# Two layers of attention and expert layers: GpSimd waits for the stores of Q and K in front of two kinds of indirect DMA

## What is computed

```python
xn = _layernorm(x, axis=-1)
x = x + _L0_attn_ref(xn, ...) + _L0_ffn_ref(xn, ...)   # experts: relu(xn W1 + b1) W2 + b2
xn = _layernorm(x, axis=-1)
x = x + _L1_attn_ref(xn, ...) + _L1_ffn_ref(xn, ...)   # experts: xn We + be
...
scores = einsum('bhqd,bhkd->bhqk', q, k) / sqrt(HD)    # attention, causal, softmax, times v, times Wo
topk_gates, topk_idx = jax.lax.top_k(gates, K)         # K = 2 of E = 8 experts
```

## Time and profile before

| | us |
|---|---|
| median of 3 executions | 3185.12 (3184.64 to 3189.36) |
| the profiled execution | 3198.38 |
| its span, first to last instruction | 3196.6 |
| PE busy in it | 3013.7 (94%) |
| DVE, ACT, POOL busy | 2392.2, 1981.2, 1024.4 |
| granted TensorE clock, mean share | 0.982 |

### The profile page before, as it was taken

How to read it: one execution, slowest core, us unless ns; L and a number is a source line. 1 busy time by engine, 2 the same in 40 slices (tenths; PEclk the granted TensorE clock), 3 DMA queues, 4 the chain that set the end, 5 groups by cost and what they waited for, 6 DMA issues and landing times.

```text
span 3196.6 us, 62083 instructions
## 1 busy us (share of the span) xinstructions
PE 3013.7 (94%) x19056; PEld 1579.7 (49%) x19056; DVE 2392.2 (75%) x7245; ACT 1981.2 (62%) x4954; POOL 1024.4 (32%) x1244
## 2 busy tenths in 40 slices
PE   5799999999999999999999999999999999999998
PEld 3454544445455554544545555454545555445443
DVE  5676768777786777878777787777877767687784
ACT  2466656666666666666666666666666666666665
POOL 4115134151432413334151331513324142241512
PEclk7899999999999999999999999999999999999999
DMA  6767455363554535446374563635546365453642
GB/s 188 201 169 209 133 157 152 107 195 110 180 184 145 184 122 176 133 130 188 100 216 139 167 182 120 190 97 166 161 132 209 120 192 153 145 156 103 185 135 77
DMA packets 328103, 496.03 MB, mean 155 GB/s; under 512 B 56832, under 2 KB 242656, under 8 KB 327776
## 3 DMA queue, kind: packets, MB, share of 16 engines
q1 hardware_dynamic: 293536, 416.99, 43.7%
q0 software_dynamic: 24576, 67.14, 6.9%
q10 hardware_dynamic: 9664, 7.93, 0.9%
HBM read 344.19 MB, written 152.84 MB: 155 GB/s over the span
## 4 chain that ended last, share of the span: by engine, by line
PE 79%; DVE 10%; issue 4%; ACT 3%; DMA 2%; SPq 1%; POOL 1%; another core or an unknown queue 0%; DVEq 0%; ACTq 0%; POOLq 0%
PE po L1144 16%; PE pmx L1094 15%; PE pst L1081 14%; PE pst L1128 9%; PE pmx L1214 5%; PE pst L1113 5%; PE pst L1225 4%; PE pmx L1183 4%; PE pst L1102 3%; DVE pmx L843 3%; DVE x L975 2%; PE pmx L1162 2%; PE pst L1150 1%; ACT probs L686 1%; DMA xg<-x_slots 1%
## 5 line engine op out<-in xcount | busy, mean ns | idle before, releaser
L686 ACT ACTIVATE probs<-pst 128x512 f32<-128x512 f32 (+3 forms) x3072 | 1402.8, 496 | 450.9 <-PE pst L1081 422.9
L595 POOL TENSOR_SCALAR_AFFINE_SELECT probs<-probs 128x512 f32<-128x512 f32 x512 | 332.5, 650 | 1686.3 <-ACT probs L686 1684.7
L839 DVE TENSOR_REDUCE rmax<-pmx 128x1 f32<-128x512 f32 x1024 | 668.9, 683 | 142.4 <-PE pmx L1094 134.5
L1081 PE MATMUL pst<-qs,k_first 98*128 98x512 bf16 (+3 forms) x2048 | 693.8, 344 | 34.3 <-ACT xgT L691 17.6
L843 DVE CUSTOM_DVE_ANT_0 pmx<-pmx,mask,rmax 128x128 f32<-128x128 f32 (+3 forms) x1024 | 537.5, 556 | 217.2 <-PE pmx L1094 189.0
L1094 PE MATMUL pmx<-k_first,qs 96*128 96x512 bf16 (+2 forms) x2048 | 672.6, 346 | 28.0 <-issue 9.3
L1144 PE MATMUL po<-probs,v 128*32 128x512 f32 (+3 forms) x6144 | 663.5, 504 | 14.6 <-POOL probs L595 10.6
L843 DVE CUSTOM_DVE_ANT_0 pmx<-pmx,mask 128x128 f32<-128x128 f32 (+3 forms) x1024 | 482.8, 510 | 168.1 <-PE pmx L1094 152.8
L1094 PEld LDWEIGHTS pmx<-k_first,qs 96*128 96x128 bf16 x2048 | 199.8, 99 | 377.8 <-issue 172.1
L1094 PE MATMUL pmx<-k_second,qs 96*128 96x128 bf16 (+3 forms) x1024 | 305.9, 303 | 28.3 <-DVE otok L955 14.5
L1081 PE MATMUL pst<-qs,k_second 98*128 98x512 bf16 (+3 forms) x1024 | 302.4, 302 | 5.8 <-issue 3.8
(11 more groups left out here) (121 smaller groups left out, 3379.9 us busy)
## 6 DMA issues: line engine op xcount, KB each, us to landing
wt<-w_tiles SPq DMA_DIRECT2D x161, 513.0 KB
qk_parts<-parts SPq DMA_DIRECT2D x256, 192.0 KB
xg<-x_slots SPq DMA_DIRECT2D x368, 128.0 KB
y_slots<-ys SPq DMA_DIRECT2D x368, 128.0 KB
wt<-w_tiles SPq DMA_DIRECT2D x184, 256.0 KB
qs<-qk_parts SPq DMA_DIRECT2D x128, 192.0 KB
qs<-qk_parts SPq DMA_DIRECT2D x128, 128.0 KB
k_first<-qk_parts SPq DMA_DIRECT2D x64, 192.0 KB, 2.9
```

Of the source, the lines that this page charges most:

```text
L595: pool.affine_select(out=tri, in_=tri, compare_op=ALU.is_ge, fill=0.0, base=0, pattern=[[0, GH], [1, P]], channel_multiplier=-1).then_inc( ...
L686: act.activation(probs[:, u % 2, j, 0:w], ps[:, 0:w], ACT.Exp, scale=DH ** -0.5).then_inc(st_read, 1)
L839: dve.tensor_reduce(rmax0[:, col:col + 1], src, AX_X, ALU.max).then_inc(mx_read, 1)
L1081: pe.matmul(ps[:, 0:w], keys[0:SROWS, j, k % HT * P:(k % HT + 1) * P], qs[0:SROWS, set_no(q, n) % QRING, j, a:a + w], start=True, stop=Tru ...
```

## The change

POOL gets two new waits, and nothing else is changed. In front of the ninth scatter it waits until all stores of tile 1 issued so far have landed, the last of which are the four of the same run's first half. In front of the first gather, in all runs but the last, it waits until all stores of tile 0 issued so far have landed, the last of which are the four of the next run's second half.

```diff
@@ scatter
                     pool.wait_ge(slots_ready, q + 1)
+                if SCATTER[a] == PROJ[0, NP - 1] + 2 and a % 2 == 0:
+                    pool.wait_ge(qk_stored[KD - 1], (q * CH + 1) * 64)
                 pool.indirect_dma_start(
@@ gather
                         pool.wait_ge(y_stored[n], 16 * (last // YRING + 1))
+                if a == 0 and q + 1 < NR:
+                    pool.wait_ge(qk_stored[0], (q + 1) * CH * 64 + 128)
                 need(pool, combined, m - GRING + 1)
```

## The result

| | before | after |
|---|---|---|
| median, us (same chip, 4 executions each) | 3187.24 | 3229.77 |
| range | 3184.64 to 3192.07 | 3223.98 to 3230.84 |
| the profiled execution | 3198.38 | 3230.84 |
| its span | 3196.6 | 3229.1 |

The ratio is 1.0128, with a 95% interval of 1.0110 to 1.0146: 42 us slower. The forecast was 3195 and its range ended at 3212. The sign was right, the size was four times too small. The profiled execution of before lies 11 us above its median and that of after 1 us above, so the two spans differ by 32.5 us where the medians differ by 42.5.

The account below looks back on a forecast made before the run. PE, busy 3013.7 of 3196.6 us, was taken to bound the kernel. The terms 8.0 us (first gather), 0 (ninth scatter, steady state) and 2.0 (start) make 10 us, so the median 3185.1 becomes 3195, range 3184 to 3212.

Parts of the forecast that it names:

- The gather's wait: On POOL in front of the first gather, at fifteen handovers: late masks of unit 44 cost PE 8.0 us together.
- From the landing to the next indirect DMA: On POOL, once the awaited stores have landed: the held gather or scatter was to start 0.15 us later.
- From the end of the issues to the landing: SP's stores of Q and K parts: landed 2.6 us after their issue, with 4.16 us as the other end.
- the slack arithmetic of the prediction: At unit 44's mask: lateness beyond PE's slack is paid in full, 0.36 us in eight handovers and 0.73 in seven.
- The scatter's wait in steady state: On POOL in front of the ninth scatter, after the start: the mask of unit 36 stays in time, costing nothing.
- the cover: POOL's 5.92 us of idle time ahead of unit 36's mask in the second run, claimed to absorb the held scatters.
- The start: Start of the program: the held ninth scatter delays PE's first tokens once, 2.0 us, between 1.3 and 2.8.
- The slack swallows it: Rival, chance 0.26: unit 44's masks are in time or PE's later waits shrink; start plus up to 4 us, 3186.5 to 3191.
- The landing comes with the last issue: Rival, chance 0.05: stores count as landed about when their issue ends, so masks are not late; 3185.
- The long landing: Rival, chance 0.10: stores land 4.16 us after the issues at each handover; 34 us slower, 3219.
- Not slower, a little faster: Rival, chance 0.09: stores and loads get the DMA engines alone, PE's 3.3 us of token waits vanish; -2 us, 3183.
- The bound on the gain: Whole kernel: stores are awaited only once, 2.1 us, in the start; faster loads can gain no more than 3.3 us.

## Why the prediction missed, step by step

**The gather's wait: the right place, 8.0 us instead of 36.** The mechanism is the one forecast, and three of its numbers were too small.

- *From the landing to the next indirect DMA* I took 0.15 us, the idle time of a gather that waited for nothing. In after it is 0.81 to 0.89 us in all fifteen handovers, mean 0.88. The held scatters show 0.74 to 0.75 in fifteen runs and 0.26 once, in the start. The row I chose showed a gather that stood ready behind another instruction, not one that a landing releases.
- *From the end of the issues to the landing* I took 2.6; the mean is 2.86 (2.43 to 3.66). Together the first gather starts 3.74 us after the issues, not 2.75.
- *Four gathers and the mask* take 5.53 us on average, not 5.30, partly because the mask itself took 0.80 in some handovers [compare rows 4].

These make each mask 1.22 us later than worked out. With that, the slack arithmetic of the prediction gives 8 x 1.58 + 7 x 1.95 = 26.3 us; measured at unit 44 are 25.0, in thirteen of the fifteen, 0.2 to 3.2 us each. One reading of the rows was wrong besides: the first and the fifteenth handover stood for two kinds, but the four issues take 3.05 to 4.11 us in the one kind and 2.65 to 3.72 in the other. Handover by handover, the forecast's own numbers give 11.0 us in place of 8.0, and with the 1.22 us added 27.0 in place of 26.3.

- *What follows a late PE* was put at nothing, without a reason. The fourteenth handover, PE, and the same place in windows of time (columns: length, busy time of PE, its loads, DVE, ACT, POOL, then the granted clock, DMA share, GB/s):

```profile
2852.95 1.07 PE L1148 MATMUL po<-probs,v 128*32 128x512 f32 x8
2858.24 1.94 PE L1148 MATMUL po<-probs,v 128*32 128x512 f32 x8 [2.64 <-POOL probs L599]
2861.15 3.34 PE L1218 MATMUL pmx<-xnT,wqk 128*128 128x512 f32 x4
```

```profile
2850.00:2855.00 5.00, 5.00 (x33) 2.35 (x30) 3.07 (x16) 3.47 (x8) 1.95 (x2) 1.00 0.59 165
2855.00:2858.00 3.00, 0.60 (x4) 0.10 (x1) 1.52 (x5) 1.34 (x4) 2.61 (x3) 0.88 0.84 227
2858.00:2861.00 3.00, 2.76 (x13) 0.91 (x14) 1.38 (x7) 0.29 (x1) 2.53 (x4) 0.50 0.95 242
2861.00:2864.00 3.00, 3.00 (x6) 1.31 (x5) 1.71 (x6) 0.46 (x2) 1.45 (x3) 0.50 0.20 49
2864.00:2867.00 3.00, 3.00 (x21) 1.59 (x20) 1.36 (x3) 1.54 (x5) 1.14 (x2) 0.99 0.30 87
```

PE had 0.60 us of work in three, waiting for the mask; then its granted clock stood at 0.50, which is 1.2 GHz instead of 2.4, and the same eight multiplications took 1.94 us where they had taken 1.07. So PE lost the wait and then lost again at half speed. In after, 13.6 us are lost this way at units 44 and 45, in six of the fifteen handovers (a wait of 2.60 us in another one was not followed by it); before had nothing of the kind there. 25.0 + 13.6 = 38.6, and the table has 38.1.

So the step that made the forecast miss is this term of the sum, 8.0 us for the wait in front of the first gather: the landing and the 0.15 us behind it were taken too short, which makes 25.0, and the half clock adds 13.6.

**The scatter's wait in steady state: 0 forecast, 42 lost and 42 given back.** That "nothing" came out near the truth is luck, two terms of 42 us that cancel. The step that failed here is "the cover is that idle time, in which POOL waits for ACT's exponentials". I measured the cover in a trace in which the units just ahead of it run slow, and held it fixed. The ninth run of before, its seventh to tenth scatters, and where PE, ACT and DVE stand around the ninth and tenth:

```profile
1608.49 0.99 POOL L570 DMA_INDIRECT x_slots<-xn,slot  x1 [0.15 <-issue]
1609.78 0.96 POOL L570 DMA_INDIRECT x_slots<-xn,slot  x1 [0.30 <-issue]
1611.05 0.96 POOL L570 DMA_INDIRECT x_slots<-xn,slot  x1 [0.30 <-issue]
1612.32 0.96 POOL L570 DMA_INDIRECT x_slots<-xn,slot  x1 [0.30 <-issue]
```

```profile
1611.26 0.44 PE L1102 MATMUL pst<-ident,xg 128*128 128x128 f32 x2
1611.54 0.22 PE L1094 MATMUL pmx<-k_second,qs 96*128 96x128 bf16 x1
...
1613.46 0.39 PE L1081 MATMUL pst<-qs,k_first 98*128 98x512 bf16 x1 [0.99 <-issue]
...
1615.13 0.39 PE L1081 MATMUL pst<-qs,k_first 98*128 98x512 bf16 x1 [1.06 <-issue]
```

```profile
1613.02 0.39 ACT L691 ACTIVATE xgT<-pst 128x256 f32<-128x256 f32 x1 [1.94 <-PE pst L1081]
```

```profile
1614.39 0.36 DVE L843 CUSTOM_DVE_ANT_0 pmx<-pmx,mask,rmax 128x128 f32<-128x128 f32 x1 [3.66 <-PE pmx L1094]
```

PE turned the tokens from 1611.26 on, 0.44 us, and ACT copies them only at 1613.02; PE did the small product at 1611.54 and DVE takes it at 1614.39. The consumers see PE's results 1.3 to 2.6 us late (counted from PE's ends, which the profile models), and then PE waits for the consumers. The same place in after, where no scatter runs:

```profile
1625.24 0.44 PE L1106 MATMUL pst<-ident,xg 128*128 128x128 f32 x2
```

```profile
1625.72 0.38 ACT L695 ACTIVATE xgT<-pst 128x256 f32<-128x256 f32 x1 [0.65 <-PE pst L1106]
```

0.04 us after PE's end. Of the 42 us at units 34 and 35, 27.2 are idle time of PE and 11.9 half clock. The pointer was in the earlier trace rows, PE's largest named wait, 17.6 us for ACT's `xgT`; I read it as one number of a list and did not ask in which unit it sat. The row is gone, or down to 1.0 us, in every run that frees units 34 and 35, and in the others it stays (14.1 us with the gather's wait alone, 13.3 with that wait at the third gather, 16.4 with waits already passed).

What the scatters need beside them for this has two readings. In all fifteen runs of before the ninth and tenth scatters stand beside the stores, and they also follow the seventh and eighth, which wait for `low_parts`, with only 0.30 us between. Every run that freed units 34 and 35 ended both. The trace of after tells them apart. Take ACT's copies of tokens and its exponentials, without the first of each unit, where ACT was idle before them: they wait for PE alone. In before 22 of 327 start over 1 us after PE's end, 19 of these in unit 34. In after none does in unit 34, but 14 of 36 in unit 36 and 4 of 5 in unit 37, around the four held scatters, and 7 of 26 in unit 44, around the four held gathers, and both go only when the stores have landed. The third run of after, where the landing is at 464.27:

```profile
465.02 0.96 POOL L572 DMA_INDIRECT x_slots<-xn,slot  x1 [6.07 <-PE pst L1085]
...
468.81 0.96 POOL L572 DMA_INDIRECT x_slots<-xn,slot  x1 [0.30 <-PE pst L1085]
```

```profile
468.31 0.33 PE L1085 MATMUL pst<-qs,k_second 98*128 98x384 bf16 x1
```

```profile
470.93 0.49 ACT L690 ACTIVATE probs<-pst 128x384 f32<-128x384 f32 x1 [1.24 <-PE pst L1085]
```

2.29 us late. With four scatters in the last step it is 14 of 17 in unit 38, and with the scatters one or two steps later, or left out, no more than 5 in the whole program and none in units 34 to 36. So these stores need not be in flight; what the late places share is a row of indirect DMAs, mostly four, one behind another. That is read off the traces: no run moved the stores and left the scatters where they were.

Once the units ahead run faster, PE needs the mask of unit 36 sooner: in the second run 12.9 us after the stores' first issue (252.30 to 265.16), where before it was 15.0 (252.86 to 267.84). The stores land no sooner, in after 3.4 to 6.2 us after the start of their fourth issue, and four scatters and the mask still have to follow. So the mask came late in twelve of the fifteen runs, 16.6 us of idle PE at unit 36, and 8.5 us are lost to half clock at units 36 and 38. It was the cover that moved: the masks of after end 12.3 to 14.4 us after the stores' first issue, and set against the 13.7 to 16.8 us that PE took in before, run by run, only one would have been late, by 0.3 us. (Nor was the second run the worst place: with the forecast's own numbers the tenth comes closest, 0.1 us beyond its slack at the upper end, which changes nothing in the sum.) The landing was no help either: 2.4 to 5.3 us after the end of the issues, in five of the fifteen runs later than the 4.16 that I took for the other end. The rest of the 42 is idle PE for the greater part as well: in units 36 to 38 it grew by 29.2 us in all, and what is not at the mask of unit 36 stands in short waits, for ACT or under "issue". The run with two scatters behind the mask shows that this is there when scatters are pressed together (24.3 us, 1.5 of them waits for masks), and the run without the four that it goes with them (-1.4).

**The start: 2.0 us forecast (1.3 to 2.8), 2.9 measured.** The mechanism and the place hold. The stores landed 4.11 us after the end of their issues (55.79), at the upper bound and not between the two; the scatter followed 0.26 later. I had split the difference, although the row of the upper bound was from this very place. Of the 6 us that the scatter's wait costs alone, 2.7 are the start.

**The rivals.** *The slack swallows it* is refuted for the first gather, and is what happens when two gathers stand in front of the wait. *The landing comes with the last issue* is refuted: the first handover's stores were first issued at 285.50 and the gather they hold starts at 292.93. An estimate of 3.8 us by the Trainium skill, page "DMA: Bandwidth & Descriptors", section "Anatomy of one DMA — SWDGE (gpsimd) path", stands against a landing some 6.6 us after the first issue (292.93 less 0.81). That section's fit is for DMAs issued by GpSimd, and SP issues these stores. The page of the profile now has the landing of one such store, known for tile 0, 3.4 us at the median:

```profile
qk_parts<-parts SPq DMA_DIRECT2D x256, 192.0 KB, 3.4
```

*The long landing* came nearest in time, 3219, but for another reason: the landing was short of 4.16 us after the issues in every handover (at most 3.66; at the ninth scatter it was not), and the time went into the 0.88 us behind it and the half clock. *Not slower, a little faster* named the tokens as the source of a gain, and no gain came from them; the gain that was there lay in units 34 and 35 and is larger than the 3.3 us which I took for the ceiling.

**The bound on the gain was the other wrong step.** "So the gain that is in reach is small" rested on the waits for the stores. The scatters slowed PE, ACT and DVE without any of them waiting for a store or a scatter by name. Taking the ninth and tenth scatters out of the stores' step, away from the seventh and eighth, is worth up to 0.8%, as the run with four scatters in the last step shows without any wait.

## What to carry to other kernels

A queue's wait is costed by what has to run between its release and the next thing that another engine needs, with the delay behind the release taken from a row that shows a release, and a cover that is read off the trace belongs to the schedule of that trace: ask whether the same change moves the engine that it is measured against. A wait of the busiest engine that is put down to an idle engine's small copy is worth opening, unit by unit, before the change is priced. And where indirect DMAs disturb the engines beside them, moving some of them by a step kept the gain here, while a wait that holds them back until something has landed released them as a burst, late.

## What the runs showed of the hardware that I had not expected

- Results of PE reach ACT and DVE 1.3 to 2.6 us late in the rows above while four scatters run one behind another; units 34 and 35 of before are 42 us longer over fifteen runs for it. It needs the scatters (left out, it is gone), and a step's distance ends it there. It does not need the 192 KB stores in flight: behind scatters and gathers that were held until these had landed, 14 of 36 copies in unit 36 and 7 of 26 in unit 44 of after were over 1 us late. By which path the indirect DMAs hold back PE's results is not settled, and no run here isolates it; since the profile models PE's ends, it is open too whether PE ends late or is heard late.
- A gather starts 0.81 to 0.89 us after the landing that releases it and a scatter 0.74 to 0.75 (0.26 once, in the start), against 0.15 to 0.30 behind another instruction.
- After 2.64 us of waiting, PE's granted clock stood at 0.50 from 2858 to 2864, and a group of multiplications took 1.94 in place of 1.07 us. In six of the fifteen handovers of after a wait of PE cost more than its length in this way.
